# First loads of a cross-attention and feed-forward kernel on one core: weights signalled one by one, position biases moved ahead, TensorE run on zeros, queries projected earlier

## The reference, cut to what matters

```python
def _aft_local(emb, wq, bq, wk, bk, wv, bv, wo, bo, pos_bias):
    q = emb @ wq + bq
    k = emb @ wk + bk
    v = emb @ wv + bv
    mask = (abs(t - j) < 64)
    w = pos_bias * mask
    ek = exp(k - max(k, axis=1))
    ew = exp(w - max(w, axis=1))
    num = einsum('tj,bjd->btd', ew, ek * v)
    den = einsum('tj,bjd->btd', ew, ek)
    y = sigmoid(q) * num / den
    return y @ wo + bo
emb  = layernorm(x) + ctx
attn = _aft_local(emb, ...)
a    = layer_norm(attn + emb, gamma, beta)
x    = x + layer_norm(relu(a @ w1 + b1) @ w2 + b2 + a, gamma, beta)
```

## Time and profile before

| | us |
|---|---|
| median of three runs | 1212.48 (1211.35 to 1216.6) |
| the profiled execution, own time | 1216.99 |
| the profiled execution, span | 1215.0 |
| TensorE busy | 1133.1, 93% of the span |
| VectorE busy | 891.0, 73% |
| ScalarE busy | 703.5, 58% |
| GpSimd busy | 351.0, 29% |

### The profile page before, as it was taken

How to read it: one execution, slowest core, us unless ns; L and a number is a source line. 1 busy time by engine, 2 the same in 40 slices (tenths; PEclk the granted TensorE clock), 3 DMA queues, 4 the chain that set the end, 5 groups by cost and what they waited for, 6 DMA issues and landing times. The chain is left out here.

```text
span 1215.0 us, 19950 instructions
## 1 busy us (share of the span) xinstructions
PE 1133.1 (93%) x6928; PEld 986.7 (81%) x6928; DVE 891.0 (73%) x1656; ACT 703.5 (58%) x1066; POOL 351.0 (29%) x343
## 2 busy tenths in 40 slices
PE   4889999988889999999999999899999999989988
PEld 3678888877679999999999888688888788768877
DVE  6988858777856556556554446999999999996575
ACT  3233334666534444444442246988988988976755
POOL 1613211622705006006000172422622612433110
PEclk9989999999999999999999999999999999998999
DMA  9200000043252453342320124232332342210011
GB/s 327 70 1 1 1 1 2 7 139 73 74 145 94 118 141 93 117 138 95 93 81 1 44 89 112 60 99 73 93 89 61 114 138 58 80 41 12 9 36 39
DMA packets 69031, 92.88 MB, mean 76 GB/s; under 512 B 16080, under 2 KB 33232, under 8 KB 68816
## 3 DMA queue, kind: packets, MB, share of 16 engines
q1 hardware_dynamic: 67328, 89.67, 25.0%
q10 hardware_dynamic: 1616, 2.10, 0.5%
HBM read 80.45 MB, written 11.14 MB: 75 GB/s over the span
## 5 line engine op out<-in xcount | busy, mean ns | idle before, releaser
L2052 DVE CUSTOM_DVE_ANT_0 at_pr<-at_sc,at_mk 128x512 f32<-128x512 f32 x256 | 165.6, 684 | 26.3 <-PE at_sc L2287 25.7
L1956 ACT ACTIVATE at_pr<-at_pr,at_nmx 128x512 f32<-128x512 f32 x256 | 170.5, 717 | 17.5 <-DVE at_nmx L2052 17.0
L2197 DVE TENSOR_TENSOR W_1l<-at_pt,W_1h 128x1024 fp32r<-128x1024 f32 x128 | 156.0, 1219 | 5.8 <-ACT W_1h L1951 5.4
L1951 ACT ACTIVATE W_1h<-at_pt 128x1024 fp32r<-128x1024 f32 x128 | 130.8, 1022 | 34.1 <-PE at_o L2321 32.4
L2302 PE MATMUL at_pt<-ident,at_pr 128*128 128x128 f32 x1024 | 135.4, 276 | 14.8 <-DVE W_1l L2197 14.1
L2302 PEld LDWEIGHTS at_pt<-ident,at_pr 128*128 128x128 f32 x1024 | 115.4, 142 | 38.1 <-issue 17.4
L229 ACT ACTIVATE moe_hs<-moe_hid,cols 128x512 f32<-128x512 f32 x120 | 82.7, 689 | 100.1 <-PE moe_hid L114 99.1
L248 DVE TENSOR_TENSOR moe_hl<-moe_ms,moe_hh 128x512 fp32r<-128x512 f32 x104 | 80.5, 774 | 64.2 <-ACT moe_hh L221 64.2
L262 DVE TENSOR_TENSOR moe_ms<-moe_hs,gate 128x512 f32<-128x512 f32 x104 | 78.4, 754 | 57.7 <-ACT moe_hs L229 56.9
L221 ACT ACTIVATE moe_hh<-moe_ms 128x512 fp32r<-128x512 f32 x104 | 65.8, 632 | 94.5 <-DVE moe_ms L262 94.5
L2321 PE MATMUL at_o<-W_1h,at_vaug 128*128 128x512 f32 x256 | 112.2, 438 | 0.3 <-DVE W_1l L2197 0.3
(11 more groups left out here) (304 smaller groups left out, 3293.0 us busy)
## 6 DMA issues: line engine op xcount, KB each, us to landing
gate<-expert_weights SPq DMA_DIRECT2D x256, 128.0 KB, 3.0
w_stage<-in_ew SPq DMA_DIRECT2D x32, 256.0 KB, 4.3
at_kp<-at_heads SPq DMA_DIRECT2D x96, 64.0 KB, 2.7
at_qp<-at_heads SPq DMA_DIRECT2D x96, 64.0 KB, 2.7
w_stage<-in_mask SPq DMA_DIRECT2D x16, 256.0 KB, 3.5
at_rb<-at_recip SPq DMA_DIRECT2D x64, 64.0 KB, 2.0
w_stage<-in_w SPq DMA_DIRECT2D x8, 256.0 KB, 8.1
w_stage<-in_sw SPq DMA_DIRECT2D x8, 256.0 KB, 3.2
```

Of the source, the lines that this page charges most:

```text
L1951: act.activation(PH[0][:, n % 2, :], PT[n % 2][:, :, :].rearrange("p c q -> p (c q)"), ACT.Copy)\
L1956: act.activation(pr_of(t)[:, x, :], pr_of(t)[:, x, :], ACT.Exp, bias=nmx[:, t % 4, x:x + 1], scale=-1.0).then_inc(s["ex"], 1)
L2052: dve.tensor_tensor_reduce(pr_of(t)[:, x, :], SB[x][:, :], mk[u // 2 % 2][:, j, :], -float(HD) ** -0.5, 3.0e38, ALU.add, ALU.min, nmx[:, t ...
L2197: dve.tensor_tensor(PH[1][:, n % 2, :], PT[n % 2][:, :, :].rearrange("p c q -> p (c q)"), f(PH[0][:, n % 2, :]), ALU.subtract).then_inc(s[ ...
```

## The change: first loads and the order around them

Seven edits, all in `early_phase`.

1. ScalarE issues keys, values, queries, output in that order, each weight on a semaphore of its own, and makes each high part when that weight has landed.
2. SyncE waits, behind the column constants, until the position biases have landed; then it issues `x` and `ctx` of the other batches, and the row constants after these.
3. GpSimd waits for the row constants ahead of the sum of the two bias rows.
4. GpSimd clears a 128x512 piece of `xh`, and TensorE runs 16 float32 matmuls of 128x256 on it, ahead of everything else; their results are overwritten later.
5. The queries of batch 0 are projected ahead of the turns of the position exponentials on TensorE; `exp_q(0)` moves ahead of `ew_high(0)` on ScalarE.
6. VectorE makes the low part of the key weights ahead of `emb_apply(0)`.
7. VectorE runs `z_low(0)` ahead of `den_times(1)`.

```diff
+WARM = 16
...
@@ SyncE
             sp.dma_start(g.cols[:, :], a["cols"]).then_inc(af["cols"], 16)
+            sp.wait_ge(af["pos"], 16)
+            sp.dma_start(g.x_res[:, TT:, :], x[:, TT:]).then_inc(af["rest"], 16)
+            sp.dma_start(g.attn[:, TT:, :], ctx[:, TT:]).then_inc(af["rest"], 16)
             sp.dma_start(g.rows[:, :, :].rearrange("p r d -> p (r d)"),
                          a["rows"].rearrange("r d -> (r d)").partition_broadcast(P)).then_inc(g.consts, 16)
-            sp.dma_start(g.x_res[:, TT:, :], x[:, TT:]).then_inc(af["rest"], 16)
-            sp.dma_start(g.attn[:, TT:, :], ctx[:, TT:]).then_inc(af["rest"], 16)
             group_dma(sp, g, 0)
@@ GpSimd
             pool.memset(g.power[:, :], -0.5).then_inc(af["pow"], 1)
+            pool.memset(xh[:, 0:2, :], 0.0).then_inc(af["zero"], 1)
...
             root_emb(1)
+            pool.wait_ge(g.consts, 16)
             pool.tensor_tensor(sb2[:, :], g.row("sb2a"), g.row("sb2b"), ALU.add).then_inc(s["sum"], 1)
@@ ScalarE
-            for j, n in enumerate(("wq0", "wk0", "wv0", "wo0")):
-                act.dma_start(wst[:, j], a[n].rearrange("(c p) n -> p c n", p=P)).then_inc(af["w"], 16)
+            for j, n in ((1, "wk0"), (2, "wv0"), (0, "wq0"), (3, "wo0")):
+                act.dma_start(wst[:, j], a[n].rearrange("(c p) n -> p c n", p=P)).then_inc(af[n], 16)
             act.dma_start(pos[:, :, :], a["pos"].rearrange("(t p) n -> p t n", p=P)).then_inc(af["pos"], 16)
-            act.wait_ge(af["w"], 64)
-            for j in (1, 2, 0, 3):
+            for j, n in ((1, "wk0"), (2, "wv0"), (0, "wq0"), (3, "wo0")):
+                act.wait_ge(af[n], 16)
                 act.activation(W[0][:, j, :, :], wst[:, j], ACT.Copy).then_inc(af["wh"], 1)
...
             exp_k(0)
+            exp_q(0)
             ew_high(0)
             ew_high(1)
-            exp_q(0)
             ew_high(2)
@@ VectorE
             dve.wait_ge(af["ctx"], 16)
-            emb_apply(0)
...
             low_weight(0, 1)
+            emb_apply(0)
             low_weight(1, 2)
...
             z_scaled(0)
+            z_low(0)
             den_times(1)
-            z_low(0)
             emb_apply(2)
@@ TensorE
+            pe.wait_ge(af["zero"], 1)
+            for _ in range(WARM):
+                pe.matmul(YB[0][:, 0:D], xh[:, 0, 0:P], xh[:, 1, :], start=True, stop=True)
             pe.wait_ge(af["id"], 16)
             turn_emb(0)
             key(0)
             value(0)
+            query(0)
             turn_ew(0)
             turn_ew(1)
-            query(0)
             turn_ew(2)
```

More of the change, by code:

```diff
@@ L482, in early_phase @@
     s = {n: sem("fr_" + n) for n in names}
-    names = ("x", "ctx", "id", "cols", "rest", "pos", "w", "wh", "wl", "pow", "band", "npm", "ew", "ewt", "ewh", "ewl", "nbq",
+    names = ("x", "ctx", "id", "cols", "rest", "pos", "wq0", "wk0", "wv0", "wo0", "zero", "wh", "wl", "pow", "band", "npm", "ew", "ewt", "ewh", "ewl", "nbq",
              "es", "em", "ev", "er", "ea", "et", "ab", "ett", "eth", "etl", "k", "v", "q", "km", "kb", "nb", "ek", "e", "ekv",
```

## The result

| | before | after |
|---|---|---|
| median of 19 runs each, us | 1214.09 | 1210.84 |
| lowest and highest, us | 1211.35, 1217.47 | 1207.77, 1213.8 |
| profiled execution, own time and span, us | 1216.99, 1215.0 | 1213.8, 1212.1 |
| ratio to before, 95% interval | | 0.9969, 0.9959 to 0.998 |

The profiled spans differ by 2.9 us. The page after has the zeros in its first row: TensorE is busier by 7.5 us, though the span is shorter, since the matmuls on zeros count as busy.

The account below looks back on a forecast made before the run. TensorE, busy 93% of the span, was taken as the bound, with its early waits setting when batch 0's denominators start. These move from 35.8 to 33.9, rounded to 2 us off the 1212.48 median: 1210.5 us, range 1206.5 to 1213.8.

Parts of the forecast that it names:

- the landing: Arrival of the position biases, which lets the first select start: 11.7 us, between 11.3 and 12.5, instead of 17.3.
- SyncE's wait: Holding other batches and row constants behind the biases costs nothing; loads resume at 13.5 us and all land by 32.3.
- The split: GpSimd's split, from 31.6 us instead of 33.71, ends at 50.0; the next root behind it has time to spare.
- The collision: Early selects on GpSimd hold VectorE's low part of the value weights to 14.4 us, so keys start at 15.75.
- The clock at the keys: After 2.85 us idle on TensorE, keys start at 1.2 GHz for some 3.1 us: 1.5 us lost, bounds 0 and 2.3.
- clock kept: Rival, chance 0.24: keys at 15.75 us at 2.4 GHz, denominators 32.4, 3.4 us gained, 1209.1 us.
- Q+8.3: Start of batch 0's denominators, 8.3 us behind the end of the queries (Q); before, it was 5.3 us.
- the one leader: Behind the projections the end of the queries, 25.6 us, leads; exponentials of biases end at 22.4, of keys at 23.7.
- the new order gives back part of the loads' gain: Projecting queries ahead of the turns of the position exponentials gives back 3 us of what the loads bring.
- clock kept, no collision: Rival, chance 0.12: value weights slip in ahead of the select, keys 14.4 us, denominators 31.0, 4.8 us gained, 1207.7.
- That shift should pass on to the end: The earlier start of batch 0's denominators, 1.9 us rounded to 2, should carry through to the kernel's end.
- The slower rival: Rival, chance 0.10: zeros on TensorE never raise the clock, end at 15.4 us, delay the turn; 1.5 us lost, 1214.0.

Follow-up runs that it names:

- e3: Kernel before plus only the load edits: weights signalled singly, position biases ahead of other loads, GpSimd's wait on the row constants; ratio to before 0.9969.
- e4: Changed kernel with SyncE issuing row constants and other batches at once, not behind the position biases; ratio to before 1.001.
- e10: Changed kernel with the position biases issued third on ScalarE's queue, ahead of query and output weights; ratio to before 0.9981.
- e2: Changed kernel with the old order of the queries on TensorE and of exp_q(0) on ScalarE; ratio to before 0.9971.
- e5: Changed kernel plus matmuls on zeros in TensorE's two waits behind the queries, four and three; ratio to before 0.9972.
- e12: e8 plus late zeros, five matmuls ahead of turn_z(0) and three behind it; ratio to before 0.9945, six executions.
- e1: Changed kernel without its sixteen matmuls on zeros; ratio to before 1.0002.
- e7: Changed kernel with den_times(1) ahead of z_low(0) again on VectorE; ratio to before 0.9986.
- e9: Changed kernel with 32 matmuls on zeros at the start instead of 16; ratio to before 1.0017.
- e8: Changed kernel with exp_q(0) back behind the second high part, emb_stats(1) behind the fourth low part, zeros in the two waits; ratio to before 0.9947.
- e6: Changed kernel with emb_stats(1) behind the fourth low part of the position exponentials on VectorE; ratio to before 0.9982.
- e11: e8 without the sixteen matmuls on zeros at the start; ratio to before 0.9962.

## Why the prediction was right, point by point

**The number and the way to it.** 1210.5 was forecast and 1210.84 measured, but part of that agreement is luck: over more runs the kernel before stands at 1214.09 and not at 1212.48, so the gain was 3.2 us where 2 had been summed. The denominators came at 33.07, forecast 33.9, and there two misses cancel: the queries ended 2.3 us earlier than forecast (23.3 instead of 25.6), and the way from there took 1.5 us longer (9.75 instead of 8.3).

**The loads.** 11.7 us was forecast for the landing, 12.5 as the upper bound; the first select started at 12.86. Two terms were too small. By 10 us the changed kernel had moved 5 x 151 + 5 x 354, 2.53 MB, and not 2.76. And by 12 us, at 389 and 311 GB/s, nearly all of the 3.25 MB had come (18 GB/s from 12 to 13), yet the select started 0.8 us later; the sum had nothing between the last bytes and the select. The lateness was lucky: it let the value weights slip in front of the select. What the prediction said of SyncE's wait holds. The split began 1.6 us later than worked out (33.25), and a cover of 5.04 us was left. e3 and e4 show that the gain hangs on the earlier biases.

**The collision.** Right as a mechanism and wrong as an event. It needs a landing before about 12; e10 brought it about, with 2.41 us for the held instruction, the figure that the earlier trace rows led to expect, and 0.7 us at the keys. In the changed kernel the low part of the value weights took 0.68 us, and this is most of why the keys came at 14.84 and not at 15.75.

**The clock at the keys.** This step failed for the profiled execution: "So I take it that the keys start at 1.2 GHz all the same". They ran at full clock. With the select out of the way the idle time behind the turn was 1.57 us and not 2.85. But the profiles of e2, e5 and e12, whose programs are the same up to the keys and whose idle time there is the same 1.57 us, lost the clock: it fell before the first key matmul in e2 and e5 and within the second in e12 (4.3 to 4.4 us from the first key to the first value, where it is 2.87 at full clock). In e4, after 2.90 us idle, it fell 0.8 us into the keys (4.43 us). So the rival "clock kept" and the forecast are both real, from one execution to the next. The last wait alone does not decide: 2.38 us in e10 kept the clock, 1.57 us in e2 lost it. What the four that lost it have in common is that their zeros were over early: the waits in front of the turn and behind it add up to 3.30 to 3.75 us in them, more than in any of the six that kept it (3.01 in the changed kernel). This is an order among ten profiles and no cause shown. Whether transposes count for the clock, as the rule of the Trainium skill that the prediction cites ("TensorE: Matmul & The Clock Gate", "Part 4: PE-mode transpose") denies, stays open: no run separates it.

**Behind the queries.** Q+8.3 was forecast; it was 9.75, and 8.2 in e1, where the clock had stayed up by itself, and in e5, where zeros held it up. Four profiles tell where the missing 1.5 us lie:

| us | changed | e7 | e10 | e1 |
|---|---|---|---|---|
| first turn to second | 3.06 | 3.06 | 2.25 | 2.25 |
| second turn to third | 3.50 | 3.50 | 3.49 | 3.49 |
| third turn to denominators | 3.35 | 3.35 | 3.36 | 2.64 |
| second and third turn take | 1.84, 1.94 | 1.22, 1.94 | 1.22, 1.94 | 1.22, 1.06 |
| queries' end to denominators | 9.75 | 9.76 | 8.94 | 8.21 |

Half of them, 0.8 us, is ScalarE and no clock: in the changed kernel and e7 the exponentials of the biases, `exp_k(0)` and `exp_q(0)` run on until after the queries' end, and the first high part starts 1.4 us behind that end (24.75 against 23.32) where 0.6 was forecast; in e10 and e1, with earlier exponentials or later queries, it is 0.6 us. The prediction had the end of the queries as the one leader. The other half, 0.7 us, is the half clock of the third turn and behind it. The half clock of the second turn costs nothing here, as e7 shows: VectorE's `emb_stats(1)` covers it. The rows of e7 and of e1:

```profile
25.95 1.22 PE L1321 MATMUL rt_r<-ident,aft_pos 128*128 128x128 f32 x8 [2.03 <-DVE W_1l L1036]
29.45 1.94 PE L1270 MATMUL rt_r<-ident,aft_pair 128*128 128x128 f32 x8 [2.27 <-DVE W_1l L1036]
```

```profile
27.29 1.22 PE L1321 MATMUL rt_r<-ident,aft_pos 128*128 128x128 f32 x8 [1.21 <-DVE W_1l L1036]
30.78 1.06 PE L1270 MATMUL rt_r<-ident,aft_pair 128*128 128x128 f32 x8 [2.27 <-DVE W_1l L1036]
```

The prediction had looked for the clock at the keys and not here, where TensorE waits more than anywhere. That the new order gives back part of the loads' gain was right in kind: 3 us were summed, and e2 shows 1.3 us at the denominators and nothing in the runs. The condition of the rival "clock kept, no collision" came in (queries' end at 23.3, forecast 22.7), but of its 4.8 us only 2.7 reached the denominators.

**What passes on.** "That shift should pass on to the end" holds: 2.73 us at the denominators, 3.58 at the first hidden, 2.9 at the end. The slower rival decided where it was said to, in e9. Edit 7 was put at nothing, and the rows under e7 show that it is nothing. Edit 6 was put at nothing too: the low part of the key weights ended at 9.17, before the root at 9.39. Its bound of 0.5 us shows in e8's profile, where the root took 1.57 us instead of 1.04 beside it and the turn of `emb` came 0.5 us late.

**The scatter.** For the changed kernel the time follows the mean granted clock: executions at 0.992 took 1207.8 to 1209.2 us, those at 0.987 took 1213.2 and 1213.8. That is about 1 us for each 0.001. Kernels with edit 5 as it stands, zeros only at the start or none (after, e1, e4, e6, e7, e9, e10), average 0.987 to 0.990; the others (before, e2, e3, e5, e8, e11, e12) 0.991 to 0.994. Edit 5 opens two waits of about 2 us on TensorE, and in the changed kernel's profile the clock is at half from 26.2 to 36.5 us. How much of the time that costs, beyond the 0.7 us behind the third turn, was not separated.

## What to carry to other kernels

When a start is bound by loads, find the one transfer whose consumers form the longest chain and hold everything else back behind it: with the weights in the order of need, that was worth as much as all seven edits, and without it the others were worth nothing. Moving work ahead of a wait on one engine is only free if the engine in front of the next step keeps its order too; here ScalarE's `exp_q`, moved along with TensorE's queries, stood in front of the work that led (0.8 us at the denominators), and putting it back was part of e8. Filling TensorE's waits with matmuls on zeros is worth trying where TensorE leads, to an amount that surely ends before the real work: sixteen too many cost 4.6 us.

## What the runs showed of the hardware that was not expected

- Matmuls on zeros do raise the clock. Sixteen of 128x256 took 8.55 to 10.20 us over nine profiles, where sixteen at half clock would take 13.8. At 0.4325 us each at full clock and twice that at half, an estimate from these numbers is 2.9 to 6.2 us at 1.2 GHz, against the 3.1 us assumed; in e10 they ended at 11.60, beyond the prediction's bound of 11.2.
- The slow stretch of the first matmuls is not in the column PEclk: in e3 it reads 1.00 from 15.5 to 19 us, where matmuls of 128x512 follow each other every 0.43 us. There the clock is to be read from the distances, and the mean granted clock leaves it out.
- The same idle time of 1.57 us in front of the keys left the clock up in five profiles (after, e6, e7, e8, e9) and down in three (e2, e5, e12); after 2.38 us it was up (e10), after 2.90 us it fell within the keys (e4). Behind the queries e1, e9 and e10 have the same two waits, 1.21 and 2.27 us, and the third turn takes 1.06 us in e1 and 1.94 in the other two. One profile does not settle what a wait costs in clock.
- An `affine_select` of 128x2048 on GpSimd keeps a VectorE subtraction with both inputs in SBUF from ending before it does: 2.41 us instead of 0.68, seen in the kernel before and again in e10.
